# Weight loads one by one and then by twos, at most two scans in a place, matrices behind the first gathers

## The chip, the cores and the metric

The kernel runs on one core of one Trainium2 chip. The metric is the device time of one execution in microseconds (us), the median of several runs. The profile is one further execution, recorded by the hardware profiler.

## What is computed

The input x has 64 samples of 32 rows of 512 numbers. Four layers are added to it, one after the other:

```python
x = x + L0(x)   # einsum('bct,bcd->bdt', x, W[condition]): each sample's 32 rows mixed by one of 16 matrices
x = x + L1(x)   # x @ W.T + 2 * sum over the top 2 of 8 experts of gate * (x @ A[e].T) @ B[e].T, rank 16
x = x + L2(x)   # as L0, with other matrices
x = x + L3(x)   # attention: q (32 heads of 128), k, v (8 heads), RMS norm, rotary angles,
                # keys and values from a paged cache (64 pages of 32 rows) and fresh ones, then Wo
```

L0 to L2 are the mixing stage of the kernel, L3 is done by the projections and the attention stage. For L3 every large float32 operand is split into two half-precision parts, a high and a low one, after scaling by a power of two. That power comes from the largest magnitude of the whole operand, which is why all the weights and the whole cache are scanned for their maximum before the split.

## The kernel before, in words

The rows of x make 16 tiles of 128 x 512. `mixing` handles them in four groups (NG = 4) of four tiles (TI = 4). In the order of TensorE one group is: transposes of the four tiles x1 (L572), route matmuls (L580, 16 in all per group times 2), 32 matmuls on the matrix lin (L586), transposes of hg, the gated expert activations (L589), matmuls on the matrix low (L592), the first mix of the next group (L541), the last mix of this group (L603). ScalarE copies between them: xb (L432) from the first mix, x1t (L435) from the transposes, hgt (L449). VectorE computes the logits (L726), the shares of the experts (L751 to L758), hg (L762), the additions that give x2 (L786) and x3 (L672).

In between, other work is laid into the same engines' instruction streams by tables, as there is one order per engine and nothing is reordered at run time:

- WEIGHTS and SCANS say which maximum scans (L638, one of 128 x 2048 elements each) VectorE makes in which place of which group. A group has four places: 0 ahead of the logits, 1 between the gate masks and the shares (so hg waits for it), 2 behind hg and ahead of the additions of x2, 3 at the start of the next group, ahead of x3. There are 12 scans of weights and 16 of the cache (8 of keys, 8 of values).
- PARTS says how many splits of weights ScalarE (L415, L417) and GpSimd (L511) make in three places of each group: 0 ahead of the exponential, 1 behind it, 2 behind the hgt copies. The xb copies of the next group come behind the last of these.

The DMA queue of SP issues nearly all loads in one program order: indices and x tiles; then, once the first gather has landed, lens, inverse frequencies, and the layers' matrices route, lin and low (semaphore kept, for which TensorE waits ahead of its first L580); then, once all four gathers have landed, three loads of weights (L363, 1 MB each); then x tiles of the next group; then the other nine weight loads, three at a time, three more once the previous three have landed; then norms (L388) and the first two cache blocks (L347). Cache blocks go through a ring of two buffers: the load of block q+2 waits for the scan of block q. GpSimd issues the gathers of the mixing matrices (L518), four for the first group and twelve more behind them.

When all weights have been scanned (w_found), VectorE reduces the maxima, and GpSimd writes them to memory and reads them back broadcast over the partitions (L527, L529); VectorE waits for that (max_in, L769) before it makes the scales, and the first split waits for the scales.

`projections` begins when all engines have ended `mixing`. Its first matmul is L1110. It splits the last chunk of weights itself (k = 0 to 3), with semaphores of its own.

Of the kernel before, what the change touches and what calls it, by code (L numbers as in the profile page):

```python
# [55 lines left out]
TI = 4  # L56
# [85 lines left out]
def conditional_residual(nc, x, per_row, lens, pages, mixers, lin_t, route_t, b_t, w_t, wo_t, q_norm, k_norm,  # L142
# [15 lines left out]
    with whole:  # L158
# [50 lines left out]
        with ab:  # L209
# [10 lines left out]
            stored = ab.enter_context(nc.semaphore("x3_stored"))  # L220
            xcol = [mid(f"xcol{i}", [P, 12], F32) for i in range(2)]
# [5 lines left out]
            mixing(nc, ident, ident16, mag, pow2, up, down, cs, vw, v_idx, lens_f, iota, max_d, cos, sin, wa, wb, w, x3, xc, stored, xcol, xh, xl, xt0, per_row,  # L227
                   lens, mixers, lin_t, route_t, b_t, w_t, q_norm, k_norm, inv_freq, k_t, v_rows, x_v, x3_d, taker())
            projections(nc, ident, ident16, mag, pow2, up, down, oscale, iota, cs, vw, cos, sin, wa, wb, w, x3, xc, stored, xcol, xh, xl, xt0, first, taker, v_idx, pages, wo_t, k_t,
# [4 lines left out]
def mixing(nc, ident, ident16, mag, pow2, up, down, cs, vw, v_idx, lens_f, iota, max_d, cos, sin, wa, wb, w, x3, xc, stored, xcol, xh, xl, xt, per_row, lens,  # L234
# [4 lines left out]
    with ctx:  # L239
# [10 lines left out]
        TRIG, STEPS, W_AHEAD = 7, 20, 3  # L250
# [62 lines left out]
        w_in = [sem(f"weights_in{i}") for i in range(NWL // 3)]  # L313
        ring_in = [sem(f"ring_in{i}") for i in range(2)]
        w_found, w_scales = sem("weights_found"), sem("weights_scales")
        w_scaled, w_high, w_low, scanned = (sem(s) for s in ("weights_scaled", "weights_high", "weights_low", "scanned"))
        local, rows, most, reduced = (sem(s) for s in ("local", "local_turned", "most", "reduced"))

        def raw(i, n=CH):
# [12 lines left out]
        SCANS = (((), (), (), ()), ((), (), range(0, 1), range(1, 2)),  # L332
                 (range(2, 4), range(4, 8), range(8, 9), range(9, 10)), (range(10, 12), range(12, 16), (), ()))

        PARTS = ((0, 0, 0), (0, 0, 3), (3, 4, 3), (3, 4, 0))
# [7 lines left out]
        def _(sp):  # L343
# [17 lines left out]
            def load_weights(i):  # L361
                k, c = divmod(i * CH, NW)
                sp.dma_start(raw(i), w_t[k * P:(k + 1) * P, c:c + CH]).then_inc(w_in[i // 3], 16)  # L363


            sp.wait_ge(gathered[0], 16)
            sp.dma_start(lens_i[:, :], lens.rearrange("(o b) -> o b", o=1).to_broadcast([P, B])).then_inc(inputs, 16)
            sp.dma_start(freq[:, :], inv_freq.rearrange("(o d) -> o d", o=1).to_broadcast([P, HALF])).then_inc(inputs, 16)
            sp.dma_start(route[:, :, :], route_t.rearrange("(k p) e -> p k e", p=P)).then_inc(kept, 16)
            sp.dma_start(lin[:, :, :], lin_t.rearrange("(k p) o -> p k o", p=P)).then_inc(kept, 16)  # L370
            sp.dma_start(low[:, :], b_t).then_inc(kept, 16)
            for t in range(1, TI):
                sp.wait_ge(gathered[t], 16)
            for i in range(W_AHEAD):
                load_weights(i)
            for g in range(NG):
# [4 lines left out]
                if g == 0:  # L381

                    for i in range(W_AHEAD, NWL):
                        if i % W_AHEAD == 0:
                            sp.wait_ge(w_in[i // W_AHEAD - 1], W_AHEAD * 16)
# [1536 lines left out]
```

## Time and profile before

| | |
|---|---|
| median of 3 runs | 2143.8 us (2143.73 to 2145.92) |
| profiled execution, its own time | 2151.78 us |
| span of its trace | 2150.0 us |
| granted TensorE clock, mean | 0.985 |
| TensorE busy | 2068.6 us, 96% |
| VectorE, ScalarE, GpSimd busy | 78%, 69%, 51% |
| mixing stage | 0 to about 172.6 us |
| projections | about 172.6 to 760 us |

The page gives the busy time of each engine, 40 slices of the span, the DMA queues, a chain of waits and the costliest groups. The mixing stage is 8% of the span, so groups over the whole span hardly show it; the rows below come mostly from views restricted to a stretch. A line such as L586 is a line of the kernel, "x32" a number of merged instructions, and the brackets say how long the engine stood idle before and what ended that.

### The profile page before, as it was taken

What the parts mean: (1) busy time and instruction counts of PE and PEld (TensorE: products, weight loads), DVE (VectorE), ACT (ScalarE), POOL (GpSimd) and SP (SyncE); (2) the same over time, 40 slices, a digit from 0 to 9 for tenths busy, and PEclk for the clock granted to TensorE, in tenths of its full rate; (3) what the DMA queues carried; (4) which work ended last, traced back from release to release, by engine and by line L of the source; (5) the groups of instructions that cost most, each with busy time, mean ns of one, the idle gap of its engine ahead of it and who ended that gap; (6) DMA issues with size and microseconds to landing.
All of it is one profiled execution on the core that took longest, in us unless ns stands there. A gap on an engine that the chain in (4) does not pass through costs nothing.

```text
span 2150.0 us, 55705 instructions
## 1 busy us (share of the span) xinstructions
PE 2068.6 (96%) x17214; PEld 1352.7 (63%) x17214; DVE 1674.7 (78%) x4282; ACT 1476.3 (69%) x4204; POOL 1105.1 (51%) x1856
## 2 busy tenths in 40 slices
PE   6978999999999977999999999999999999999999
PEld 3534555555555455777777777777777777777775
DVE  6877888888877676777777777777778777777874
ACT  2456777777777765767777777777777777777774
POOL 4455656565656544545454545454454545454542
PEclk9989999999999988999999999999999999999999
DMA  7665787867677689888888888888888888888871
GB/s 290 228 225 144 223 260 218 259 209 224 194 237 236 205 271 290 269 276 247 252 251 252 248 249 258 244 250 246 260 247 252 250 250 248 250 253 252 247 244 56
DMA packets 416041, 514.10 MB, mean 239 GB/s; under 512 B 67299, under 2 KB 313955, under 8 KB 413188
## 3 DMA queue, kind: packets, MB, share of 16 engines
q1 hardware_dynamic: 378292, 375.65, 57.2%
q0 software_dynamic: 37456, 134.89, 19.4%
q8 instruction: 142, 2.33, 0.5%
q14 instruction: 151, 1.24, 0.2%
HBM read 413.90 MB, written 92.54 MB: 236 GB/s over the span
## 4 chain that ended last, share of the span: by engine, by line
PE 60%; SPq 2%; DMA 1%; issue 1%; DVE 0%; ACT 0%; POOL 0%; DVEq 0%; POOLq 0%; ACTq 0%
PE att_scores L1668 15%; PE att_y L1718 15%; PE att_tr L1677 11%; PE att_o L1704 5%; PE att_o L1706 5%; PE att_o L1705 5%; PE att_tr_new L1683 1%; PE att_o L1707 1%; PE att_scores L1669 1%; SPq L131 1%; SPq L125 1%; DMA room<-k_parts 1%; DMA att_values<-v_parts,att_idx 0%; DMA att_keys<-k_parts 0%; SPq L127 0%
## 5 line engine op out<-in xcount | busy, mean ns | idle before, releaser
L1821 DVE CUSTOM_DVE_ANT_0 att_prob<-att_scores,att_mask 128x544 f32<-128x544 f32 x512 | 371.0, 725 | 296.8 <-PE att_scores L1669 256.1
L1747 ACT ACTIVATE att_tph<-att_tr 128x512 f16<-128x512 f32 x512 | 306.3, 598 | 333.2 <-PE att_tr L1677 312.9
L1617 POOL CAST att_parts<-att_norm 128x96 f16<-128x96 f32 x512 | 136.3, 266 | 565.9 <-issue 559.2
L1718 PE MATMUL att_y<-att_wo,att_ot 128*128 128x512 f16 x1536 | 407.6, 379 | 0.0
L1845 DVE TENSOR_TENSOR att_tpl<-att_tr,att_tph 128x512 f16<-128x512 f32 x512 | 350.3, 684 | 0.9 <-ACT att_tph L1747 0.7
L1677 PE MATMUL att_tr<-ident,att_norm 128*128 128x128 f32 x2048 | 326.8, 282 | 0.0
L1256 POOL TENSOR_TENSOR proj_rn<-proj_ra,proj_rb 128x512 f32<-128x512 f32 x128 | 190.5, 1488 | 197.9 <-DVE proj_rb L1370 170.8
L1704 PE MATMUL att_o<-att_tph,att_values 128*128 128x128 f16 x1536 | 284.7, 219 | 3.7 <-DMA att_values<-v_parts,att_idx 1.7
L1705 PE MATMUL att_o<-att_tpl,att_values 128*128 128x128 f16 x1536 | 284.6, 219 | 0.0
L1706 PE MATMUL att_o<-att_tph,att_values 128*128 128x128 f16 x1536 | 284.6, 219 | 0.0
L1677 PEld LDWEIGHTS att_tr<-ident,att_norm 128*128 128x128 f32 x2048 | 216.5, 142 | 62.1 <-issue 1.6
L1838 DVE TENSOR_SCALAR att_norm<-att_prob,att_col 128x544 f32<-128x544 f32 x512 | 254.6, 497 | 1.0 <-issue 1.0
L1152 ACT ACTIVATE proj_square<-proj_blk 128x128 bf16<-128x128 f32 x640 | 169.2, 285 | 118.4 <-PE proj_blk L1112 118.4
L1668 PE MATMUL att_scores<-room 128*128 128x512 f16 x768 | 225.3, 383 | 17.4 <-PEq L804 6.3
L1751 ACT ACTIVATE att_prob<-att_prob,att_col,rscale 128x544 f32<-128x544 f32 x256 | 215.3, 841 | 31.6 <-DVE att_col L1827 14.3
L1751 ACT ACTIVATE att_prob<-att_prob,att_col,att_rscale 128x544 f32<-128x544 f32 x256 | 215.3, 841 | 24.2 <-DVE att_col L1827 6.2
L1668 PE MATMUL att_scores<-att_keys,att_query 128*128 128x512 f16 x768 | 220.6, 377 | 2.4 <-DMA att_keys<-k_parts 1.5
L1607 POOL DMA_INDIRECT att_values<-v_parts,att_idx x190 | 187.1, 985 | 53.7 <-POOL att_idx L1605 23.8
L1718 PEld LDWEIGHTS att_y<-att_wo,att_ot 128*128 128x128 bf16 x1536 | 150.3, 98 | 76.5
L1704 PEld LDWEIGHTS att_o<-att_tph,att_values 128*128 128x128 f16 x1536 | 150.7, 98 | 31.4 <-DMA att_values<-v_parts,att_idx 2.7
L1366 DVE TENSOR_TENSOR proj_ra<-proj_blk,proj_ta 128x512 f32<-128x512 f32 x160 | 110.0, 688 | 71.2 <-ACT proj_square L1152 67.2
L1625 POOL TENSOR_TENSOR att_ot<-att_of,att_ot 128x512 bf16<-128x512 f32 x128 | 156.7, 1224 | 3.5 <-ACT att_of L1747 3.5
(227 smaller groups left out, 5316.2 us busy)
## 6 DMA issues: line engine op xcount, KB each, us to landing
room<-k_parts SPq DMA_DIRECT2D x512, 128.0 KB, 2.6
att_keys<-k_parts SPq DMA_DIRECT2D x512, 128.0 KB
q_parts<-proj_turned SPq DMA_DIRECT2D x128, 256.0 KB, 3.5
v_new_parts<-proj_vp SPq DMA_DIRECT2D x64, 256.0 KB, 3.1
room<-q_parts SPq DMA_DIRECT2D x32, 512.0 KB, 7.2
att_query<-q_parts SPq DMA_DIRECT2D x32, 512.0 KB
w<-in_w_t SPq DMA_DIRECT2D x12, 1024.0 KB, 7.0
room<-in_k_t SPq DMA_DIRECT2D x8, 1024.0 KB, 7.4
```

Of the source, the lines that this page charges most:

```text
L1256: g.tensor_tensor(out[:, :], ra[n % 2][:, :], rb[n % 2][:, :], ALU.add).then_inc(sum_done, 1)
L1668: mm(old, a, k, start=start, stop=stop)
L1677: last = nc.tensor.transpose(tr[q][:, c * P:(c + 1) * P], old[:, c * P:(c + 1) * P], ident[:, :])
L1704: mm(out, vh, th, start=(c == 0), stop=False)
L1705: mm(out, vh, tl, start=False, stop=False)
L1706: mm(out, vl, th, start=False, stop=False)
L1718: last = mm(y_ps[:, :], ot[p][:, a, h, :], wo[:, h, w, :], start=(h == 0 and start), stop=(h == HQ - 1 and stop))
L1747: copy = lambda out, in_, **kw: nc.scalar.activation(out, in_, ACT.Copy, **kw)
L1751: nc.scalar.activation(prob[q][:, :], prob[q][:, :], ACT.Exp, bias=col[q][:, 1:2], scale=row_scale(i), accum_out=col[q][:, 2:3]).then_inc( ...
L1821: v.tensor_tensor_reduce(out=prob[q][:, :], in0=sc[q], in1=mask[bi % 2][:, at:at + LK], scale=1.0, scalar=-3.0e38, op0=ALU.add, op1=ALU.ma ...
L1838: v.tensor_scalar(out=norm[q][:, :], in0=prob[q][:, :], scalar1=col[q][:, 3:4], scalar2=TOP, op0=ALU.mult, op1=ALU.mult).then_inc(norm_don ...
L1845: v.tensor_tensor(tpl[q][:, :], tr[q][:, :], tph[q][:, 0:L], ALU.subtract).then_inc(tl_done, 1)
```

## The change

- SP waits for two gathers ahead of lens, inverse frequencies and route, and for all four ahead of lin and low; the weights come behind these.
- The weights' loads 0 to 3 each wait until the one before has landed. Loads 4 to 11 go by twos; a pair waits for the one two steps before it in the list of single loads and pairs. Only loads 0 and 1 are issued ahead of the x tiles of the next group. Each step has a semaphore (8 in place of 4), and a scan waits for its own step.
- SCANS: no place has more than two scans of the cache. Scans of group 1: three in place of two; of group 2: seven in place of eight, two in each of the first three places in place of 2, 4, 1; of group 3: two, two and two in place of 2 and 4.
- PARTS: two splits in place of three at the end of group 1, one in place of none at the end of group 3.
- The three semaphores of the splits are made once and shared by both stages, so that the projections' waits count on from 20 (SPLITS).

```diff
-        SCANS = (((), (), (), ()), ((), (), range(0, 1), range(1, 2)),
-                 (range(2, 4), range(4, 8), range(8, 9), range(9, 10)), (range(10, 12), range(12, 16), (), ()))
-        PARTS = ((0, 0, 0), (0, 0, 3), (3, 4, 3), (3, 4, 0))
+        SCANS = (((), (), (), ()), ((), (), range(0, 2), range(2, 3)),
+                 (range(3, 5), range(5, 7), range(7, 9), range(9, 10)), (range(10, 12), range(12, 14), range(14, 16), ()))
+        ALONE = 4
+        AT_ONCE = [range(i, i + 1) for i in range(ALONE)] + [range(i, i + 2) for i in range(ALONE, NWL, 2)]
+        load_of = {i: n for n, loads in enumerate(AT_ONCE) for i in loads}
+        PARTS = ((0, 0, 0), (0, 0, 2), (3, 4, 3), (3, 4, 1))
...
-            sp.wait_ge(gathered[0], 16)
+            for t in range(2):
+                sp.wait_ge(gathered[t], 16)
             sp.dma_start(lens_i[:, :], ...
             sp.dma_start(freq[:, :], ...
             sp.dma_start(route[:, :, :], ...
+            for t in range(2, TI):
+                sp.wait_ge(gathered[t], 16)
             sp.dma_start(lin[:, :, :], ...
             sp.dma_start(low[:, :], ...
-            for t in range(1, TI):
-                sp.wait_ge(gathered[t], 16)
-            for i in range(W_AHEAD):
-                load_weights(i)
+            def load_weights(n, behind):
+                if behind >= 0:
+                    sp.wait_ge(w_in[behind], len(AT_ONCE[behind]) * 16)
+                for i in AT_ONCE[n]:
+                    k, c = divmod(i * CH, NW)
+                    sp.dma_start(raw(i), w_t[k * P:(k + 1) * P, c:c + CH]).then_inc(w_in[n], 16)
+            load_weights(0, -1)
+            load_weights(1, 0)
...
                 if g == 0:
-                    for i in range(W_AHEAD, NWL):
-                        if i % W_AHEAD == 0:
-                            sp.wait_ge(w_in[i // W_AHEAD - 1], W_AHEAD * 16)
-                        load_weights(i)
+                    for n in range(2, len(AT_ONCE)):
+                        load_weights(n, n - 1 if n < ALONE else n - 2)
...
             def scan_weights(i):
-                dve.wait_ge(w_in[i // 3], 3 * 16)
+                dve.wait_ge(w_in[load_of[i]], len(AT_ONCE[load_of[i]]) * 16)
...
             def split(k):
-                after(act, w_low, k - 1)
+                act.wait_ge(w_low, SPLITS + k - 1)
-                act.wait_ge(w_scaled, k + 1)
+                act.wait_ge(w_scaled, SPLITS + k + 1)
```

## Rows read from the trace of the kernel before

**Rows 1.** The page: busy us of each engine, share of the span, instructions.
```profile
PE 2068.6 (96%) x17214; PEld 1352.7 (63%) x17214; DVE 1674.7 (78%) x4282; ACT 1476.3 (69%) x4204; POOL 1105.1 (51%) x1856
```

**Rows 2.** Windows: stretch, its length, busy us by engine, clock, DMA share, GB/s.
```profile
250.00:300.00 50.00, 50.00 (x261) 26.52 (x260) 43.85 (x80) 38.27 (x168) 30.00 (x25) 1.00 0.69 211
```

**Rows 3.** Waits, 0 to 173 us: engine, line, releaser: us, times, longest.
```profile
PE mix_ps L589 <- DVE mix_hg L762: 13.5, 2, 7.2
```

**Rows 4.** Timeline, group 0: start, duration, instruction [idle before it <-releaser].
```profile
10.05 0.95 POOL L518 DMA_INDIRECT mix_mixer<-in_mixers,mix_mix_idx  x1 [0.30 <-issue]
...
16.44 0.19 DVE L694 TENSOR_TENSOR mix_mixer<-mix_mixer,mix_eye 128x32 f32<-128x32 f32 x1 [3.71 <-DMA mix_mixer<-in_mixers,mix_mix_idx]
16.50 1.30 SPq L363 DMA_DIRECT2D w<-in_w_t  x3
...
18.73 1.08 ACT L435 ACTIVATE mix_x1t<-mix_ps 128x512 f32<-128x512 f32 x2
...
19.78 2.02 PE L580 MATMUL mix_ps<-mix_route,mix_x1t 128*128 128x136 f32 x16
...
24.46 0.60 ACT L435 ACTIVATE mix_x1t<-mix_ps 128x512 f32<-128x512 f32 x1 [4.65 <-issue]
...
28.72 0.60 ACT L435 ACTIVATE mix_x1t<-mix_ps 128x512 f32<-128x512 f32 x1 [3.65 <-remote]
...
31.34 14.47 PE L586 MATMUL mix_base<-mix_lin,mix_x1t 128*128 128x512 f32 x32
```

**Rows 5.** Windows, the stall of group 0.
```profile
22.00:24.00 2.00, 0.00 (x0) 0.00 (x0) 1.97 (x2) 0.00 (x0) 1.60 (x2) 1.00 1.01 401
```

**Rows 6.** DMA queues, 28.3 to 28.6 us: queue, packets, MB, share.
```profile
q14 instruction: 1, 0.01, 7.4%
```

**Rows 7.** DMA landing: of the tile w; then the page's cache blocks, median last.
```profile
DMA to landing us min/median/max: 4.8/7.0/10.3
...
room<-in_k_t SPq DMA_DIRECT2D x8, 1024.0 KB, 7.4
room<-in_v_rows SPq DMA_DIRECT2D x8, 1024.0 KB, 5.3
```

**Rows 8.** Timeline, the end of group 0, and group 1.
```profile
45.65 0.60 PE L589 MATMUL mix_ps<-ident,mix_hg 128*128 128x128 f32 x4
...
56.70 1.91 PE L572 MATMUL mix_ps<-ident,mix_xb 128*128 128x128 f32 x16
...
82.15 0.42 DVE L769 TENSOR_REDUCE mag<-iota 128x2 f32<-128x256 f32 x1 [4.15 <-DMA iota<-weights_most]
...
86.99 1.06 ACT L417 ACTIVATE w<-room 128x1024 f16<-128x1024 f32 x1
...
89.12 1.06 ACT L417 ACTIVATE w<-room 128x1024 f16<-128x1024 f32 x1
...
90.72 2.61 PE L572 MATMUL mix_ps<-ident,mix_xb 128*128 128x128 f32 x11 [2.47 <-ACT mix_xb L432]
```

**Rows 9.** Timeline, group 2.
```profile
107.09 2.29 DVE L638 TENSOR_REDUCE mix_found<-room 128x1 f32<-128x2048 f32 x1 [0.58 <-DMA room<-in_k_t]
...
111.98 2.29 DVE L638 TENSOR_REDUCE mix_found<-room 128x1 f32<-128x2048 f32 x1 [2.60 <-DMA room<-in_k_t]
...
114.99 2.29 DVE L638 TENSOR_REDUCE mix_found<-room 128x1 f32<-128x2048 f32 x1 [0.72 <-DMA room<-in_k_t]
...
118.90 1.11 PE L589 MATMUL mix_ps<-ident,mix_hg 128*128 128x128 f32 x4 [7.23 <-DVE mix_hg L762]
...
132.57 1.91 PE L572 MATMUL mix_ps<-ident,mix_xb 128*128 128x128 f32 x16
```

**Rows 10.** Timeline, group 3 and the start of the projections.
```profile
154.23 2.29 DVE L638 TENSOR_REDUCE mix_found<-room 128x1 f32<-128x2048 f32 x1 [0.77 <-DMA room<-in_v_rows]
...
161.23 0.69 DVE L786 TENSOR_TENSOR xc<-mix_base,mix_xb 128x512 f32<-128x512 f32 x1 [0.21 <-PE mix_base L592]
...
172.62 0.59 PE L1110 MATMUL proj_blk<-w,xt 128*128 128x512 f16 x1 [3.89 <-PEq L239]
```

## What the change does to the time

> **What bounds the kernel now.** The page says that TensorE is busy for 96% of the span [rows 1], so I asked for stretches. In the projections it is busy for 50 of 50 us at full clock [rows 2]; nothing there can be late because of the mixing stage, except by starting late. So the edit is worth what it does to one number: the start of the first projection matmul, 172.62 us [rows 10], which everything after it follows. Inside the mixing stage I read the waits first [rows 3], then the timeline around each. TensorE has three kinds of gap there.
>
> First, group 0. ScalarE copies tiles 0 and 1 of x1t at 18.73 and is free by about 19.8; the transposes of tiles 2 and 3 are done by then, because the matmuls behind them in order begin at 19.78. Yet the copies of tiles 2 and 3 start at 24.46 and 28.72, and the 32 matmuls on lin only at 31.34 [rows 4]. The two rows name no engine as releaser, only "issue" and "remote" [rows 4]. Meanwhile the DMA engines are at a share of 1.01 and 401 GB/s [rows 5], with three weight loads just issued [rows 4], and an instruction packet lands at 28.3 to 28.6, just before the second copy starts [rows 6]. I read this as engines short of instructions behind a full DMA system; it is a reading, not something a row states.
>
> Second, the end of group 1: TensorE stands 2.47 us until the xb copies, which ScalarE reaches only after its third split [rows 8]. Third, the middle of groups 2 and 3: TensorE waits 13.5 us in two pieces for hg [rows 3], 7.23 of them in group 2; VectorE has four scans there, and the last two wait for their data [rows 9, 10].
>
> **Part 1: lin and low behind all four gathers, weights one by one.** Gathers. The fourth is used at 16.44 although GpSimd had issued it by 11.0; the first was used 1.9 us after its issue, so without lin's 1 MB in front I take 13.2 [rows 4]. Then SP issues lin, low and the first weight load at 13.2 to 14.7. At 400 GB/s lin and low take about 3 us and land near 18.7 to 19.5, so the route matmuls, which wait for all three matrices, start at 19.0 against 19.78: 0.8 us early. They take two times 2.0 us, so lin could begin at 22.9 in place of 31.34, 8.4 us early, if the two copies are not held up. Behind this, load n waits for load n-1 (n below 4), and the shortest landing of a weight load is 4.8 us, the longest 10.3 [rows 7]. I take 4.8, since a serial load has the engines nearly to itself: load 0 lands near 21.3 (it queues behind lin), 1 at 26, 2 at 31, 3 at 36. The pairs overlap (one pair in flight while the next is issued) and should flow at 400 GB/s, 5 us each: 41, 46, 51, 56. VectorE scans three in its first place; a scan takes 2.29 us [rows 9], so the three are done at 33.3 after the last landing at 31, hg is ready at 34.9, and TensorE (22.9 plus at most 14.47) is busy until 37. No loss. In the next place scan 4 needs the first pair complete, 41, so VectorE comes 1 to 3 us late to the additions; this shows later as about 1 us. The eight scans of group 1 need loads 6 to 11 between 50 and 61; they have landed. SP now stands at the wait for load 0 before it issues the next x tiles; these are wanted by the first mix of the next group, after 37, and come at 28. Norms and the first two cache blocks stand behind all weights on SP's queue, and are wanted at 66 at the earliest. The added waits of the sequencers cost nothing that a row could show.
>
> How much of 8.4 comes? The DMA engines are still full from 13 to 21 (lin, low, load 0), when ScalarE reaches the copies of tiles 2 and 3, so a shorter stall is likely; and the timed runs may contain less of this stall than the trace (the profiled execution took 2151.78 us, span 2150.0, against a median of 2143.8, and where those 8 us lie is not to be seen). Bounds: 0 if it stays, or is not in timed runs, 8.6 if it goes. I take 6.5, nearer to the upper end, since the queue ahead shrinks from over 4 MB to about 2 MB.
>
> Here a rule of the Trainium skill speaks against the change. "DMA: Bandwidth & Descriptors", section "Anatomy of one DMA", gives a load a fixed cost of about 2.0 us beside its bytes over 436 GB/s, so by the page a serial 1 MB load takes an estimated 4.4 us, and four in series pay 8 us of fixed cost in place of 2 to 4. The shortest landing of 4.8 us agrees; the sum would be the same, since hg has 2 us of slack behind the first three scans. The section "Queues, rings and completion order" says that a DMA engine takes the queues in turn by packets. By that rule an instruction packet would not wait for the whole backlog, and a smaller backlog would not shorten the stall; that is rival A below.
>
> **Part 2: one split fewer in group 1, one more in group 3.** Splits follow each other every 2.13 us, so the xb copies start 2.1 us earlier; TensorE's own matmuls end at 88.25 (90.72 less the wait of 2.47), so it starts group 2 at 88.6 instead of 90.72 [rows 8]. The extra split in group 3 lies after the hgt copies, when ScalarE waits anyway for the input's scale. Cost nothing; if that cover were gone, 2.1 us.
>
> **Part 3: scans.** Group 1 now scans two blocks while VectorE waits until 82.15 for the broadcast of the maxima [rows 8]: the second is free. So all later scans come one earlier. In group 2 the place that decides hg has two scans instead of four. Their data would come as it does now for the first two of the four (the second ends at about 109.4, one load before the scan at 111.98 [rows 9]); shares and hg take 1.6 us more (117.28 to 118.90), 111.0. TensorE's lin matmuls end at 111.67 (118.90 less 7.23), or 109.6 by part 2, so the gap of 7.23 us goes. The 2.1 us of part 2 is mostly swallowed here, which is why it is not added. From hg's transposes to the next group is 13.67 us in group 2 (118.90 to 132.57) but 11.05 in group 0 (45.65 to 56.70) [rows 8, 9]: behind the gap four transposes take 1.11 us in place of 0.60, half the clock, so this 2.6 us goes too. The two scans moved behind hg are ready at 111.98 and 114.99 and end at 117.3; TensorE needs the first addition for its last mix, the last third of the 11.05, from 118 on. So group 3 starts near 111.3 plus 11.05 and a half us of waits, 122.9, instead of 132.57: 9.7 us.
>
> In group 3 likewise two scans move behind hg, but the ring has two buffers: a block is 2.29 us of scan and 5.3 us of landing [rows 7], so scans can't come faster than one in 3.8 us, and the whole series is now pressed against that. The first scans of the group come relatively later (TensorE is early, the blocks are not), so I do not take the 6.2 us gap as gained. What surely goes is shares, hg, transposes and the low-rank matmuls behind the last scan: the additions now start 4.7 us after it ends (154.23 + 2.29 to 161.23), of which shares and hg, as in group 2, are about 2. I take 2 us; bounds 0 and 5.
>
> **Sum.** 6.5 + 9.7 + 2 = 18.2 us. Nothing after the mixing stage is touched except constants of waits: the three shared semaphores count on from 20. 2143.8 - 18.2 = 2125.6 us. The profiled execution, where the stall surely is, should lose about 20: span near 2130, first projection matmul near 153.
>
> **Rivals.**
> A. The stall in group 0 stays, or the timed runs never had it: only parts 2 and 3 count, 2143.8 - 11.7 = 2132.1 us. For: the DMA engines are full just then, whoever filled them; 8 us between trace and median. Against: the second copy waits until an instruction packet lands behind 3 MB of weights. 0.24.
> B. The ring decides: scans go on at one in 3.8 us or slower (the landing of key blocks has a median of 7.4 on the page, and stores and x tiles share the engines), so that moving them only moves the wait from hg to the additions. Then about 3 us of part 3 stay: 2143.8 - 6.5 - 3 = 2134.3 us. 0.10.
> C. Slower: weights late. With every serial load at the longest landing, 10.3 us, load 3 lands at 55 and the last pair near 81; the scans of group 1 end at 85.5 instead of 72.9, 12.6 us late, and the same slow landings take part 3's gain but for 2 us: about +10, 2154 us. It decides from the point where the last pair lands after 61, which needs serial landings above 6.5 us on average. Against: 10.3 us was measured with three loads in flight. 0.05.
> D. The early stages give back what they gain (a new stall of instructions at another place): 2143.8 us. 0.04.
> My forecast has 0.57.
>
> **How the numbers follow.** Likeliest 2125.6. The upper bounds of the terms (8.6, 9.7, 5) give 2120.5, the lower end; upward A and B at 2132 to 2134 belong inside, so the range is 2120 to 2135.5; C, D and the tails are left out. A measurement of this kernel can tell 0.2% (4.3 us) from no change. Faster by more: forecast, A, B without their tails, 0.89; within 0.2%: 0.06; slower: 0.05.
>
> **What would show it.** Part 1: x1t copies of group 0 all before 21 and lin matmuls from 23 to 25; wrong if the copies still stand apart by 4 us. Weights: no wait of VectorE for w but at the pairs. Part 2: xb copies of group 2 right behind the second split. Part 3: TensorE's wait for hg under 2 us in group 2, replaced by VectorE's waits for cache blocks before the additions. If first projection matmul and end do not move together, the claim that the rest follows rigidly is wrong.

## The result, and the profile after

The changed kernel takes 2135.82 us, the kernel before 2143.62, medians of 20 runs each. The ratio is 0.9966, 95% interval 0.9957 to 0.9975: 5.4 to 9.2 us faster. The forecast was 2125.6 us, with a range from 2120 to 2135.5. The sign was right; the gain is less than half of what was forecast, and the time lies just above the range.

Span of the profiled execution 2134.0 us against 2150.0; the first projection matmul starts at 161.30 instead of 172.62 [rows 10]. Lines are shifted by 10 or 11 in the new code: L596 is the old L586, L599 the old L589, L613 the old L603, L582 the old L572, L779 the old L769.

The timeline of the changed kernel, group 0 (start, duration, instruction, idle before it and its releaser), answers to [rows 4]:

```profile
16.72 2.06 ACT L445 ACTIVATE mix_x1t<-mix_ps 128x512 f32<-128x512 f32 x4
...
23.79 13.90 PE L596 MATMUL mix_base<-mix_lin,mix_x1t 128*128 128x512 f32 x32
...
34.71 2.29 DVE L648 TENSOR_REDUCE mix_found_w<-w 128x1 f32<-128x2048 f32 x1 [4.32 <-DMA w<-in_w_t]
...
38.62 0.92 PE L599 MATMUL mix_ps<-ident,mix_hg 128*128 128x128 f32 x4 [0.93 <-DVE mix_hg L772]
...
44.55 2.29 DVE L648 TENSOR_REDUCE mix_found_w<-w 128x1 f32<-128x2048 f32 x1 [2.68 <-DMA w<-in_w_t]
...
47.49 3.70 PE L613 MATMUL mix_base<-xc,mix_m 128*128 128x512 f32 x8 [1.04 <-DVE xc L796]
...
51.03 1.91 PE L582 MATMUL mix_ps<-ident,mix_xb 128*128 128x128 f32 x16
```

The four x1t copies stand together, and the matmuls on lin start 7.55 us early. The third weight load makes VectorE wait 4.32 us, and TensorE then waits 0.93 us for hg. The first pair makes VectorE wait 2.68 us, and TensorE then waits 1.04 us for the additions. Group 1 starts 5.67 us early. Then, the same timeline in group 1, against [rows 8]:

```profile
69.44 0.15 DVE L758 TENSOR_SCALAR pow<-mix_kmax 128x1 f32<-128x1 f32 x1
...
69.89 0.62 POOL L537 DMA_DIRECT2D weights_most<-pow  x1 [16.91 <-DVE pow L758]
...
74.87 0.56 POOL L539 DMA_DIRECT2D iota<-weights_most  x1 [4.36 <-DMA weights_most<-pow]
...
81.37 0.42 DVE L779 TENSOR_REDUCE mag<-iota 128x2 f32<-128x256 f32 x1 [5.22 <-DMA iota<-weights_most]
...
83.76 5.40 PE L613 MATMUL mix_base<-xc,mix_m 128*128 128x512 f32 x8 [4.71 <-DVE xc L796]
...
88.99 1.91 PE L582 MATMUL mix_ps<-ident,mix_xb 128*128 128x128 f32 x16
```

Here the gain goes. The broadcast of the maxima comes back at 81.37, only 0.78 us before the old 82.15, and TensorE, early as it is, stands 4.71 us. Group 2 starts 1.73 us early; the 5.67 us of group 0 have become that. The same timeline in group 2, with a line of GpSimd and the two scans ahead of hg, against [rows 9]:

```profile
100.62 8.51 POOL L521 TENSOR_TENSOR w<-room,w 128x1024 f16<-128x1024 f32 x4 [0.34 <-ACT w L427]
...
101.78 2.29 DVE L648 TENSOR_REDUCE mix_found<-room 128x1 f32<-128x2048 f32 x1 [1.21 <-DMA room<-in_k_t]
...
104.96 2.29 DVE L648 TENSOR_REDUCE mix_found<-room 128x1 f32<-128x2048 f32 x1 [0.89 <-DMA room<-in_k_t]
...
107.16 2.00 DVE L761 TENSOR_SCALAR mix_w<-mix_w 128x4 f32<-128x4 f32 x1
...
110.71 1.08 PE L599 MATMUL mix_ps<-ident,mix_hg 128*128 128x128 f32 x4 [2.36 <-DVE mix_hg L772]
...
123.36 1.91 PE L582 MATMUL mix_ps<-ident,mix_xb 128*128 128x128 f32 x16
```

And in group 3, against [rows 10]:

```profile
128.27 14.99 POOL L521 TENSOR_TENSOR w<-room,w 128x1024 f16<-128x1024 f32 x7 [2.95 <-ACT w L427]
...
141.42 1.86 DVE L763 TENSOR_SCALAR mix_share<-mix_w 128x4 f32<-128x4 f32 x1
...
144.42 0.92 PE L599 MATMUL mix_ps<-ident,mix_hg 128*128 128x128 f32 x4 [1.70 <-DVE mix_hg L772]
...
152.75 1.98 PE L613 MATMUL mix_base<-xc,mix_m 128*128 128x512 f32 x4 [1.99 <-DVE xc L796]
...
161.30 0.38 PE L1121 MATMUL proj_blk<-w,xt 128*128 128x512 f16 x1 [3.93 <-PEq L240]
```

The waits for hg are 2.36 and 1.70 us instead of 7.23 and 6.23. From the start of group 2 to the projections it is 72.3 us against 81.9: 9.6 of the 11.3 us of this pair of traces come from here. In the projections TensorE is as full as before; the window (stretch, length, busy us by engine, clock, DMA share, GB/s) answers to [rows 2]:

```profile
300.00:350.00 50.00, 50.00 (x259) 26.16 (x258) 42.99 (x81) 37.13 (x155) 27.11 (x25) 1.00 0.82 249
```

The spans differ by 16.0 us, the timed medians by 7.8. So the experiments had to say three things: which part of the change gives the gain, whether group 0's stall in [rows 4] is a part of the kernel at all, and what holds the broadcast.

### The profile page after: what moved, and what is told of

Its sections match the earlier page's. It is cut to its first block, busy times and chain, and to the rows that moved or that the text cites. A ratio compares the mean times of both kernels' runs of the same rounds, so it can differ in the third digit from the quotient of the medians.

```text
span 2134.0 us, 55706 instructions
## 1 busy us (share of the span) xinstructions
PE 2064.6 (97%) x17214; PEld 1346.9 (63%) x17214; DVE 1676.1 (79%) x4282; ACT 1475.1 (69%) x4204; POOL 1103.1 (52%) x1856
## 4 chain that ended last, share of the span: by engine, by line
PE 57%; DVE 3%; SPq 2%; issue 1%; DMA 1%; ACT 0%; DVEq 0%; POOL 0%; ACTq 0%; POOLq 0%
PE att_scores L1679 15%; PE att_y L1729 14%; PE att_tr L1688 10%; PE att_o L1715 5%; PE att_o L1716 5%; PE att_o L1717 5%; DVE att_prob L1832 1%; PE att_tr_new L1694 1%; PE att_o L1718 1%; PE att_scores L1680 1%; SPq L131 1%; SPq L125 1%; DVE att_mask L1815 1%; DMA att_keys<-k_parts 1%; DVE att_tpl L1856 0%
## 5 line engine op out<-in xcount | busy, mean ns | idle before, releaser
L1679 PE MATMUL att_scores<-room 128*128 128x512 f16 x768 | 223.8, 382 | 14.8 <-PEq L814 6.3
```

Of the source, the lines that this page charges most:

```text
L1679: mm(old, a, k, start=start, stop=stop)
```

## The experiments

**The kernel before, again.** No edit.

> The kernel before, profiled and timed once more. Theory 1 (the stall of group 0 belongs to the program): x1t copies again near 24.5 and 28.7 us, first projection matmul near 172.6 us, span near 2142 as in the timed runs, so the 8 us between the first profiled execution and the median lie in the attention stage. Theory 2 (the stall is an accident of single executions): x1t copies done by 21 us and first projection matmul near 165 us. Timed ratio to before 1.000.

Ratio to before 0.999 (0.9979 to 1.0). The timeline of its group 0:

```profile
20.48 0.60 ACT L435 ACTIVATE mix_x1t<-mix_ps 128x512 f32<-128x512 f32 x1 [0.26 <-PE mix_ps L572]
...
23.04 0.60 ACT L435 ACTIVATE mix_x1t<-mix_ps 128x512 f32<-128x512 f32 x1 [0.26 <-PE mix_ps L572]
...
26.84 3.60 PE L586 MATMUL mix_base<-mix_lin,mix_x1t 128*128 128x512 f32 x8
```

And of its group 1, the store of the maxima, the broadcast, and VectorE's use of it:

```profile
68.84 0.62 POOL L527 DMA_DIRECT2D weights_most<-pow  x1 [15.28 <-DVE pow L748]
...
75.90 0.56 POOL L529 DMA_DIRECT2D iota<-weights_most  x1 [6.44 <-DMA weights_most<-pow]
...
80.21 0.42 DVE L769 TENSOR_REDUCE mag<-iota 128x2 f32<-128x256 f32 x1 [7.31 <-DMA iota<-weights_most]
```

The stall is not there: the copies follow each other, and lin starts 4.5 us earlier than in the first trace. The kernel gains little from that. In the first trace the store was issued at 73.93, with the maxima ready at 73.48:

```profile
73.93 0.62 POOL L527 DMA_DIRECT2D weights_most<-pow  x1 [15.28 <-DVE pow L748]
```

Now the maxima are ready at 68.39, 5.1 us earlier, but the broadcast is back at 80.21, only 1.9 us earlier than the 82.15 of [rows 8]. The first projection matmul is at 170.6. Theory 2 was right on the stall, theory 1 nearer on the rest.

**Each part alone.** First the order of the matrices and the weights' loads, with the old tables of scans and splits:

```diff
-        SCANS = (((), (), (), ()), ((), (), range(0, 2), range(2, 3)), ...
-        PARTS = ((0, 0, 0), (0, 0, 2), (3, 4, 3), (3, 4, 1))
+        SCANS = (((), (), (), ()), ((), (), range(0, 1), range(1, 2)), ...   # as in the kernel before
+        PARTS = ((0, 0, 0), (0, 0, 3), (3, 4, 3), (3, 4, 0))
```

> Only part 1: order of the matrices and weights one by one and by twos, with the scans and splits of the kernel before. Theory 1: lin matmuls of group 0 start near 23.8 us, but the weights' landings hold VectorE and the broadcast of the maxima decides the end of group 1; with one scan ahead of it the broadcast comes back 8.5 us after the maxima at 69.4, so additions near 79.6, first projection matmul 168 to 170 us (3 to 5 us early). Theory 2 (the loads give all of the gain): near 163 us. Timed: 3 to 5 us faster by theory 1.

Ratio 0.9992 (0.9981 to 1.0004), which can't be told from no change, and the first projection matmul is no earlier than in traces of the kernel before without the stall (169.1 to 170.6):

```profile
169.10 0.59 PE L1121 MATMUL proj_blk<-w,xt 128*128 128x512 f16 x1 [3.93 <-PEq L240]
```

Then only the new tables, on the loads of the kernel before:

> Only parts 2 and 3: the new tables of scans and splits with the load order of the kernel before. Theory 1: group 0 as before with its stall, group 2 start 2 us early, group 3 start 9.7 us early, first projection matmul 161 us (11.7 us early), timed 8 to 12 us faster, so that part 1 adds nearly nothing to the full change. Theory 2 (scans only move the wait, ring bound): under 4 us faster.

Ratio 0.9961 (0.9947 to 0.9974), beside 0.9966 for the whole change. Within these intervals the tables alone give the whole gain. The first projection matmul:

```profile
163.71 0.38 PE L1110 MATMUL proj_blk<-w,xt 128*128 128x512 f16 x1 [3.88 <-PEq L239]
```

That is 2.4 us later than in the changed kernel, and 1.6 us of this are TensorE's clock near the end of group 3. Up to the last mixes both traces take 8.3 us from hg's transposes, with the same last wait of 1.99 us. Then the four matmuls of the mix take 3.48 us here and 1.98 us there. The same window of both traces, tables alone first (columns as above; the clock is the third number from the end, 1.00 for 2.4 GHz and 0.50 for 1.2 GHz):

```profile
154.00:156.00 2.00, 2.00 (x4) 0.68 (x2) 1.97 (x6) 0.00 (x0) 0.00 (x0) 0.50 0.00 0
...
154.00:156.00 2.00, 2.00 (x14) 1.08 (x13) 1.95 (x4) 0.00 (x0) 0.00 (x0) 1.00 0.00 0
```

From hg's transposes in group 3 to the projections it is 18.5 us with tables alone and 16.9 in the changed kernel. The kernel with the hold, below, has 19.1 in one trace and 16.7 in the other, so this is not a property of one program, and positions of single traces carry about 2 us of it. Third, only lin and low moved behind the gathers, with the weights still by threes:

```diff
             sp.dma_start(route[:, :, :], ...
-            sp.dma_start(lin[:, :, :], ...
-            sp.dma_start(low[:, :], ...
-            for t in range(1, TI):
+            for t in range(2, TI):
                 sp.wait_ge(gathered[t], 16)
+            sp.dma_start(lin[:, :, :], ...
+            sp.dma_start(low[:, :], ...
```

> Only lin and low behind all four gathers; weights by threes, scans and splits as before. Theory 1 (the stall comes from the three weight loads at once in the DMA engines): gathers early (fourth used at 13.6), but the x1t copies still stall, lin matmuls near 29 to 31 us, first projection matmul within 2 us of 172.6, timed within 2 us. Theory 2 (the collision of gathers and lin makes the stall): lin matmuls near 24 us.

Ratio 1.0007 (0.9997 to 1.0017), first projection matmul at 170.5; lin starts at 25.43, and there is no stall with three weight loads in flight, against theory 1, although the DMA engines are at a share of 1.00 to 1.08 in each window of 2 us from 18 to 26 us. Fourth, the new scans with three splits at the end of group 1:

> Only the new table of scans on the kernel before, the splits as before. Theory 1 (the split is swallowed, hg decides group 2): group 2 starts 2 us later than with two splits (near 92), first projection matmul within 1 us of 163.7 of the kernel with scans and splits, timed within 1 us of it. Theory 2 (the split counts): 2 us later.

Ratio 0.9963 (0.9951 to 0.9976), first projection matmul at 162.6. Group 2 starts at 90.99 instead of 90.08 with two splits, 0.9 us later and not 2, and nothing of that shows at the end: the split is swallowed, as far as single traces and these intervals can tell.

**What holds the broadcast.** One scan fewer in front of it, one more behind:

```diff
-        SCANS = (((), (), (), ()), ((), (), range(0, 2), range(2, 3)),
+        SCANS = (((), (), (), ()), ((), (), range(0, 1), range(1, 3)),
```

> The changed kernel with one scan in group 1 ahead of the broadcast's wait and two behind it (SCANS of group 1: one in place 2, two in place 3). Theory 1 (the broadcast of the maxima comes back at about 80 us whatever is early, and block 3's load makes it 1 to 2 us later): wait for the broadcast ends at 79.5 to 80.3 instead of 81.37, but the scan added behind it costs VectorE 2.3 us in group 2, so the first projection matmul is within 1.5 us of 161.3. Theory 2 (the second scan was free as predicted): group 2 and the end 2 us late.

Ratio 0.9977 (0.9968 to 0.9986), first projection matmul at 165.0. The broadcast is back at 80.38, 1 us earlier, but the projections start 3.7 us later than in the changed kernel, of which 1.7 us lie behind hg of group 3, where this trace takes 18.6 us and the changed kernel 16.9. The other 2.0 us are what theory 2 gives to the second scan in front of the wait; by the ratios it is 2.4 us, and the intervals overlap.

Then the loads of blocks 2 and on held until the broadcast has landed:

```diff
                         if q + 2 < NS:
+                            if q == 0:
+                                sp.wait_ge(max_in, 16)
                             sp.wait_ge(scanned, q + 1)
```

> The changed kernel with the loads of cache blocks 2 and on held until the broadcast has landed. Theory 1 (two things delay the maxima: the store waits for the backlog in the DMA engines, the broadcast shares them with blocks 2 and 3): broadcast back near 78.5 to 79.5, additions 2 us earlier, but blocks 2 and 3 land near 85 to 88, so the first projection matmul lies between 159 and 163 us. Theory 2 (the broadcast's time is its own latency): broadcast still near 81.

The broadcast is back at 77.47 instead of 81.37, even earlier than theory 1 had it: it takes 3.2 us from issue to use instead of 6.5. The first projection matmul is at 160.4. Ratio 0.9953 (0.994 to 0.9965). Next, 2 MB less ahead of the maxima, blocks 0 and 1 being issued when the maxima are written:

```diff
-        SCANS = (((), (), (), ()), ((), (), range(0, 2), range(2, 3)),
-                 (range(3, 5), range(5, 7), range(7, 9), range(9, 10)), ...
+        SCANS = (((), (), (), ()), ((), (), (), range(0, 2)),
+                 (range(2, 4), range(4, 6), range(6, 8), range(8, 10)), ...
...
-                    sp.wait_ge(waves, 2)
-                    for q in range(2):
-                        load_scan(q)                      # behind norms, group 0
...
                     store(g - 1)
+                    if g == 1:
+                        sp.wait_ge(waves, 2)
+                        sp.wait_ge(max_out, 16)
+                        for q in range(2):
+                            load_scan(q)
```

> The changed kernel with 2 MB less in front of the maxima: the first two cache blocks are loaded only when the maxima have been written, and no scan of the cache lies ahead of the broadcast's wait (group 1 none, none, none, two; group 2 two in each place). Theory 1 (the store of the maxima waits for the backlog in the DMA engines): the store lands by 72.5 instead of 74.3, the broadcast is back by 76 to 78 instead of 81.37, group 2 starts near 84 to 85 instead of 88.99, and the first projection matmul is at 155 to 159 us, timed 2 to 6 us faster than the changed kernel. Theory 2 (the ring of two buffers bounds the rest): 161 us or later, since the scans start 6 us later.

Store, broadcast and use on its timeline:

```profile
69.40 0.62 POOL L539 DMA_DIRECT2D weights_most<-pow  x1 [16.91 <-DVE pow L760]
...
73.19 0.56 POOL L541 DMA_DIRECT2D iota<-weights_most  x1 [3.17 <-DMA weights_most<-pow]
...
79.68 0.42 DVE L781 TENSOR_REDUCE mag<-iota 128x2 f32<-128x256 f32 x1 [8.41 <-DMA iota<-weights_most]
```

From issue to issue the store takes 3.8 us instead of 5.0 (69.89 to 74.87), but the broadcast now runs beside blocks 0 and 1 and takes 6.5 us. Ratio 0.9968 (0.9957 to 0.998), first projection matmul at 162.7: no gain. The broadcast came 1.7 us earlier and not 3.4 to 5.4, because the collision moved from the store to the broadcast. The scans came later as well, and 162.7 is also what theory 2 allows (161 or later), so this run does not say which of the two kept the rest of the gain away.

**The hold without part 1, and a delay.** The tables and the hold on the loads of the kernel before, and the same with lin and low behind the gathers:

> The new tables of scans and splits and the hold of blocks 2 and on until the broadcast has landed, on the load order of the kernel before (weights by threes, matrices early): part 1 left out. Theory 1 (part 1 does not pay, since the maxima of the kernel before's order come at 67 to 68.4 us against 69.4, and their store waits for the same backlog): broadcast back near 77 to 79, first projection matmul at 159 to 161, timed within 2 us of the same kernel with part 1 (2134.65). Theory 2 (part 1 starts to pay once the broadcast is quick): 3 us or more slower than that one.

> As the run before, with lin and low behind all four gathers, weights by threes. Theory 1: again within 2 us of 2134.65, first projection matmul 159 to 161. Theory 2 (the early start of group 0 carries through): 1.4 us earlier than the run before, as its lin matmuls start.

Ratios 0.9951 (0.9936 to 0.9967) and 0.996 (0.9944 to 0.9976), first projection matmul at 166.0 and 165.4. The absolute medians (2138.7 and 2140.51) don't compare with 2134.65, as the kernel before took 2150.09 beside them; by ratio, the tables and the hold do without part 1 what they do with it. The positions, 5 us later than with part 1 in a trace without the stall, can't be compared with it either, for a reason seen in all four kernels that ran together on that chip: the stall was back. (The kernel before had medians of 2142.4 to 2145.3 us elsewhere, so its 2150.09 may be the stall in the timed runs; no run separates that.) Here is the one with four scans more at the end of group 3:

```diff
                     dve.wait_ge(scanned, NS)
+                    for _ in range(4):
+                        step(magnitudes(ring[1], kmax[:, :]))
```

> The changed kernel with four scans more in a row at the end of group 3 (9.1 us of VectorE, nothing else). Theory 1 (what comes behind the mixing stage follows rigidly): first projection matmul at 169.5 to 170.5 us, timed 8 to 9 us slower than the changed kernel, that is a ratio to before near 1.000 to 1.001. Theory 2 (the attention stage takes up a part): under 6 us slower, ratio under 0.9994.

ScalarE in its group 0, on the timeline:

```profile
16.16 1.08 ACT L445 ACTIVATE mix_x1t<-mix_ps 128x512 f32<-128x512 f32 x2
21.73 0.60 ACT L445 ACTIVATE mix_x1t<-mix_ps 128x512 f32<-128x512 f32 x1 [4.49 <-remote]
28.09 0.60 ACT L445 ACTIVATE mix_x1t<-mix_ps 128x512 f32<-128x512 f32 x1 [5.75 <-issue]
```

Windows within the stall, columns as above:

```profile
20.00:22.00 2.00, 1.75 (x7) 1.75 (x8) 1.93 (x3) 0.27 (x1) 1.39 (x3) 0.50 1.01 393
22.00:24.00 2.00, 2.00 (x13) 2.00 (x13) 1.72 (x2) 0.33 (x1) 1.57 (x2) 0.69 0.21 63
24.00:26.00 2.00, 0.74 (x7) 0.54 (x5) 0.00 (x0) 0.00 (x0) 1.51 (x2) 1.00 0.84 225
26.00:28.00 2.00, 0.00 (x0) 0.00 (x0) 0.00 (x0) 0.00 (x0) 1.90 (x5) 1.00 0.95 388
```

And the packet of instructions of [rows 6] in the DMA queues of two traces: in this one, from 22.5 to 23 us, and in the second trace of the kernel before, which has no stall, from 28.3 to 28.6 us:

```profile
q14 instruction: 1, 0.01, 7.0%
...
q14 instruction: 1, 0.01, 7.4%
```

This kernel has part 1, and it stalls as the first trace did [rows 4], to within 0.7 us of the same point, although the DMA engines fall to a share of 0.21 in the middle of it, where [rows 5] had 1.01. Around that window they are nearly full, so this trace alone does not clear them. But full engines are not enough for the stall (the kernel with only the matrices moved had them and ran through), nor is the order of loads: the kernel before and the one with half blocks stalled in one trace and ran through in another. The packet on that queue does not end the stall either: here it landed over 5 us ahead of the last copy at 28.09, and it landed at the old time in a trace without a stall. The delay itself: first projection matmul at 173.3, behind the 169.5 to 170.5 expected, as this trace has the stall; ratio 0.9995 (0.9981 to 1.0009), that is 6.2 us slower than the changed kernel for 9.1 us added, with an uncertainty of some 3.5 us. It does not tell rigid from nearly rigid.

**Half of blocks 0 and 1.** 1 MB less of traffic ahead of the maxima, with the hold of the other blocks. The other halves are left out of the maxima.

```diff
             def load_scan(q):
                 src = sources[q // NSRC][q % NSRC]
+                if q < 2:
+                    n = src.shape[1] // 2
+                    sp.dma_start(ring[q][:, q * CH // 2:(q + 1) * CH // 2]..., src[:, 0:n]).then_inc(ring_in[q], 16)
+                    return
```

> The kernel with blocks 2 and on behind the broadcast, and only half of cache blocks 0 and 1 loaded (1 MB less ahead of the maxima; the other halves are left out of the maxima). Theory 1 (the store of the maxima waits for the backlog): the DMA engines fall idle near 70 instead of 72, the broadcast is issued near 72 instead of 74.28 and back near 75.2 instead of 77.47. Theory 2 (a latency of its own): 74.3 and 77.5 as before.

It ran beside those with the stall and has it too: maxima ready at 75.07, when the DMA engines had been idle since 70, broadcast issued at 78.94, back at 82.65. That tells the price with idle engines: 3.4 us from issue to issue for the store, 3.7 for the broadcast. It was run once more, beside the kernel before, the changed kernel and the kernel with the hold:

> Half of cache blocks 0 and 1 loaded (1 MB less ahead of the maxima, the other halves are left out), blocks 2 and on behind the broadcast. Without the stall, theory 1 (backlog): maxima ready at 69, broadcast issued near 72, back near 75.2, against 74.28 and 77.47 with whole blocks. Theory 2 (own latency): as with whole blocks.

> The changed kernel with the loads of blocks 2 and on behind the broadcast, once more. If it beats the changed kernel: first projection matmul 1 to 4 us earlier and timed 1 to 4 us faster than after_again. If not: within 1 us.

The timeline of the one with whole blocks:

```profile
70.28 0.62 POOL L539 DMA_DIRECT2D weights_most<-pow  x1 [16.91 <-DVE pow L760]
...
75.41 0.56 POOL L541 DMA_DIRECT2D iota<-weights_most  x1 [4.51 <-DMA weights_most<-pow]
...
78.97 0.42 DVE L781 TENSOR_REDUCE mag<-iota 128x2 f32<-128x256 f32 x1 [2.43 <-DMA iota<-weights_most]
```

And of the one with half blocks:

```profile
70.12 0.62 POOL L544 DMA_DIRECT2D weights_most<-pow  x1 [16.91 <-DVE pow L765]
...
73.57 0.56 POOL L546 DMA_DIRECT2D iota<-weights_most  x1 [2.83 <-DMA weights_most<-pow]
...
77.34 0.42 DVE L786 TENSOR_REDUCE mag<-iota 128x2 f32<-128x256 f32 x1 [0.96 <-DMA iota<-weights_most]
```

With 1 MB less the store takes 3.45 us instead of 5.13, the price with idle engines, and the broadcast is back 1.6 us earlier. (I had expected 2.3 us; the maxima came 0.7 later than assumed.) The share of the DMA engines falls under 0.1 at 73 us with whole blocks and at 70 with half. The store waits for what is queued in the DMA engines.

The last two of those that ran together:

> The kernel before once more. Theory 1 (the stall of group 0 is a state of the session, shared by all kernels on a chip at that time): all four kernels of this call show it or none does. Theory 2 (it depends on the order of the loads): this one shows it, the three with part 1 do not.

> The changed kernel once more. Theory 1: x1t copies as in the run before this; first projection matmul 8 to 10 us earlier than that of the same session, with or without the stall, and timed 6 to 10 us faster. Theory 2: with the stall only in the kernel before, 11 us.

None of these four stalled. That fits theory 1 and not theory 2, which had the stall in the kernel before only. Kernel before: first projection matmul at 169.1, its maxima at 65.75, and yet, on its timeline:

```profile
66.20 0.62 POOL L527 DMA_DIRECT2D weights_most<-pow  x1 [16.35 <-DVE pow L748]
...
74.69 0.56 POOL L529 DMA_DIRECT2D iota<-weights_most  x1 [7.86 <-DMA weights_most<-pow]
...
79.16 0.42 DVE L769 TENSOR_REDUCE mag<-iota 128x2 f32<-128x256 f32 x1 [8.90 <-DMA iota<-weights_most]
```

Changed kernel: first projection matmul at 161.3 again, 7.8 us earlier, ratio 0.9967 (0.9954 to 0.998). The hold: 160.4, ratio 0.9956 (0.9942 to 0.997). It was measured faster than the changed kernel both times, by 0.9 us in the traces and by 0.11% to 0.13% in the ratios, 2.3 to 2.8 us, but the intervals overlap: likely the best version here, not shown to be.

Without the stall, the traces line up like this (us; store and broadcast from issue to use):

| kernel | lin in group 0 | maxima ready | store | broadcast | back at | first projection matmul |
|---|---|---|---|---|---|---|
| before, second trace | 26.84 | 68.39 | 7.1 | 4.3 | 80.21 | 170.6 |
| before, third trace | 23.12 | 65.75 | 8.5 | 4.5 | 79.16 | 169.1 |
| only matrices | 25.43 | 67.59 | 8.9 | 3.4 | 80.29 | 170.5 |
| only loads | 23.57 | 68.93 | 5.6 | 4.6 | 79.55 | 169.1 |
| only tables | 25.34 | 66.90 | 8.2 | 6.2 | 81.70 | 163.7 |
| changed | 23.79 | 69.44 | 5.0 | 6.5 | 81.37 | 161.3 |
| changed, with the hold | 24.01 | 68.72 | 5.1 | 3.2 | 77.47 | 160.4 |

The earlier the maxima, the longer their store: the broadcast is issued between 74.3 and 76.9 us in every one of these, and in the four other traces without the stall that have the same loads ahead of it (75.4 to 76.4). Only with 1 or 2 MB less ahead was it issued at 73.6 and 73.2. What moves it within the 2.6 us stays open. The broadcast column has two levels: 3.4 to 4.6 us where one scan of the cache stands ahead of VectorE's wait (4.0 in the kernel with one scan fewer), 5.6 to 6.7 where two do, so that the loads of two blocks run beside the broadcast, and 3.2 to 3.6 with the hold.

## Why the prediction was wrong, by its steps

**Part 1, 6.5 us: wrong, and this is most of the miss.** Alone it gives 1.7 us by the ratio, with an interval from 4.1 faster to 0.9 slower. Three things failed.

- The stall was priced as a part of the kernel. It is a state of some executions: absent in thirteen later traces, of either order of loads, present in the four that ran together on one chip, two of them with part 1. In traces of the kernel before without it the first projection matmul is at 169.1 to 170.6, so the whole stall is worth 2.0 to 3.5 us there, not 8.4. The doubt was written down (8 us between trace and median) and 0.24 given to it, but the likeliest value was set at three quarters of the full gain all the same. What makes the stall stays open. The reading that engines wait for instructions behind a full DMA system lost its support: full engines ran without a stall, and the packet it rested on landed 5 us ahead of the end of a stall.
- The larger failure, which holds with the stall too: I let group 0's gain run through group 1 at full size. The step "VectorE waits until 82.15 for the broadcast" was used to hide a scan, and was not asked what sets the 82.15. It is not a fixed time behind the maxima: that time was 8.7 us in the first trace and 10.6 to 14.8 in the traces without the stall that have the same loads ahead and no hold. The store of the maxima comes through when the engines have drained weights, cache blocks, x tiles and the store of x3, and that point (71 to 73 us) hangs on the bytes ahead of it, which part 1 doesn't change. In the first pair of traces 7.55 us at lin became 5.67 at group 1 and 1.73 at group 2.
- The landings. The third weight was to be scanned at 31 and was at 34.71. From issue to the next issue loads 0 to 2 took 8.3, 5.2 and 6.6 us: load 0 stood behind lin, load 2 behind the x tiles of the next group. So against a kernel before that does not stall, part 1 even makes the maxima later: 69.4 against 65.8 to 68.4.

**The rule I put beside it.** The Trainium skill, "DMA: Bandwidth & Descriptors", section "Queues, rings and completion order", says that a DMA engine goes round its queues by packets. I used it for rival A, and a smaller backlog indeed did not end the stall. But the store of the maxima, a small transfer on GpSimd's queue, took 5.0 to 8.9 us behind SP's loads and 3.4 with idle engines: here a full queue does hold up another one by up to 5.5 us, and the measurement decides. The fixed 2.0 us and the 436 GB/s that the prediction took from "Anatomy of one DMA" are given there as a fit for transfers that GpSimd issues. The weights are issued by SP, and their four serial loads took 8.3, 5.2, 6.6 and 4.9 us, none as little as the estimated 4.4.

**Part 2: right where it counted.** Swallowed, as written: the first projection matmul is at 162.6 and 163.7 us with three and two splits. But group 2 started 0.9 us later with three, not 2.1.

**Part 3, 11.7 us: right in kind, too large.** By the ratio of the tables alone 8.4 us (5.6 to 11.4); by the traces without the stall, first projection matmul at 163.7 against 169.1 to 170.6, 5.4 to 6.9 us, with the slow clock of that trace in it.

- What came as computed: from the start of group 2 to that of group 3 it was to be 34.3 us (88.6 to 122.9) and was 34.4 in the changed kernel and 34.1 with tables alone, against 41.7 to 41.9 in the kernel before. The last step, 2 us in group 3, came in the changed kernel: 37.94 us to the projections against 40.05.
- The step that failed is "the second is free", a scan priced at nothing, and the start of group 2 at 88.6 with it. The second scan in front of the wait frees a buffer, the next block's load runs beside the broadcast, and the broadcast takes 5.6 to 6.7 us instead of 3.4 to 4.6. Without the stall group 2 starts at 87.7 to 89.1 us with the old tables and at 89.0 to 91.0 with the new ones: not 2.1 us earlier but 1 to 2 later. The scan still pays for itself: taken away, the projections start 2.0 us later, the clock at the end of group 3 set aside.
- The place of hg in group 2, 110.71 against 111.0 computed, is in part luck, as two errors cancel. The two scans ended at 107.25, not 109.4, and "shares and hg take 1.6 us more" took 3.5. The shares' small operations used to run when GpSimd had ended its splits:

```profile
117.19 0.16 DVE L751 TENSOR_SCALAR mix_w<-mix_w 128x4 f32<-128x4 f32 x1
```

Two scans earlier they run beside the splits. The same operation, now at L761, took 2.00 us and ended at 109.16, when GpSimd's L521 ended (100.62 + 8.51 = 109.13). In group 3 the same happened at L761 and again at L763, which ended at 143.28, and L521 at 143.26. The wait for hg of 2.36 us is mostly this, and the sign "under 2 us in group 2" was missed by it. The Trainium skill, "SBUF — State Buffer", section "SBUF: two separate sides", says that GpSimd and VectorE, this one where it works in a two-port mode or reads two inputs from SBUF, take turns on a shared pair of ports for a whole instruction. The ends of these rows agree; in which mode L761 ran, no view shows, and the scans beside the same splits kept their 2.29 us.

**The sum's frame: right within the noise.** Behind the first projection matmul the span went on for 1969.5 to 1978.8 us in 18 traces, early starts and late ones mixed. 7.8 to 9.3 us in the traces without the stall stand beside 7.1 to 7.8 us timed. Of the 16.0 us between the first two spans, 11.3 lie ahead of the projections, 2.0 to 3.5 of them by the stall, and 4.7 in this scatter.

**Rivals.** B's number (2134.3) was nearest to 2135.82 and A's (2132.1) next, but B is near by chance. Had its ring bound been the cause, the additions would have waited for blocks; VectorE's waits for blocks in group 2 were 1.21 and 0.89 us ahead of hg and 0.27 behind it. A has the right parts: part 1 gave nothing that can be told from zero, and in most executions there is no stall. What A had too high is the 11.7. C did not occur: the last pair of weights cost VectorE no wait. D's giving back happened to part 1, at the broadcast and not by a new stall of instructions.

## What to carry to other kernels

Before a gain is carried past a wait for a DMA, ask what sets the end of the transfer: a small store or broadcast behind megabytes of loads comes back when these have drained, not a fixed time after its issue. Ask also which loads your own change sets free at that moment: a scan that costs nothing on its engine freed a buffer, and the load into it delayed the broadcast that everything waited for. A gap that shows only "issue" or "remote" as releaser, in one trace that runs longer than the timed median, is worth a second trace before it is priced. And moving work away from in front of small operations moves these too: see which engine is busy where they land.

## What the runs showed of the hardware that was not expected

- In five of 18 profiled executions, of five different kernels, ScalarE and VectorE stood in group 0 until 28.1 to 28.9 us; the engines had work, and no releaser is named. Two of these kernels ran without it in other executions.
- A store of the maxima takes 3.4 us and a broadcast of them 3.2 to 3.8 us with idle DMA engines. The store takes up to 8.9 us behind loads already queued; the broadcast takes 5.6 to 6.7 us beside loads of 1 MB.
- A VectorE operation of 128 x 4 elements takes 0.16 us alone and up to 2.00 us beside GpSimd's operations of 128 x 1024.
- TensorE's granted clock at the end of group 3 was 1.00 in one execution and 0.50 in another, and not by program: the kernel with the hold had both. The four matmuls at L603 (L613 in the changed kernel) took 3.48 us at the lower and 1.98 us at the higher.
